# Mixture-of-experts stage of a four-layer network on one core: transposes by DMA in place of TensorE

## What is computed

```python
logits = xf @ gate_inp.T
topv, topi = jax.lax.top_k(logits, K)             # K = 4 of E = 16 experts
w = jax.nn.softmax(topv, axis=-1)
u = jnp.einsum('nc,ehc->neh', xf, W_up)           # C = 256, H = 448
g = jnp.einsum('nc,ehc->neh', xf, W_gate)
h = jax.nn.silu(g) * u
y = jnp.einsum('neh,ech,ne->nc', h, W_down, dense_w)
```

## Time and profile before

| | |
|---|---|
| median of 3 runs | 2166.65 us |
| profiled execution, own time | 2164.68 us |
| its span in the profile | 2162.4 us |
| PE busy | 1870.4 us, 86% |
| DVE busy | 1362.2 us, 63% |
| POOL busy | 825.9 us, 38% |
| ACT busy | 761.3 us, 35% |

### The profile page before, as it was taken

How to read it: one execution, slowest core, us unless ns; L and a number is a source line. 1 busy time by engine, 2 the same in 40 slices (tenths; PEclk the granted TensorE clock), 3 DMA queues, 4 the chain that set the end, 5 groups by cost and what they waited for, 6 DMA issues and landing times. The chain is left out here.

```text
span 2162.4 us, 35897 instructions
## 1 busy us (share of the span) xinstructions
PE 1870.4 (86%) x9588; PEld 1324.7 (61%) x9589; DVE 1362.2 (63%) x3020; ACT 761.3 (35%) x1527; POOL 825.9 (38%) x823
## 2 busy tenths in 40 slices
PE   3589999999999999989999988637999999999990
PEld 2367766766666756667766756525666666666660
DVE  3778887877887877878877874213444444444445
ACT  3334434434434434434434432212222222232323
POOL 2123333332242332243332230124555555555554
PEclk7799999999999999999999998869999999999995
DMA  8223123123133223133123120068333333333337
GB/s 282 61 78 105 52 86 102 53 83 102 43 94 102 58 78 102 41 94 103 50 87 102 46 78 24 15 213 254 59 58 63 59 59 59 59 59 60 59 53 238
DMA packets 155390, 187.60 MB, mean 87 GB/s; under 512 B 38672, under 2 KB 134224, under 8 KB 154960
## 3 DMA queue, kind: packets, MB, share of 16 engines
q1 hardware_dynamic: 110288, 115.44, 17.1%
q0 software_dynamic: 40704, 67.40, 15.4%
q10 hardware_dynamic: 4352, 4.20, 0.6%
HBM read 119.23 MB, written 67.73 MB: 86 GB/s over the span
## 5 line engine op out<-in xcount | busy, mean ns | idle before, releaser
L1619 PE MATMUL pu<-w_ug,xh 128*128 x1728 | 361.7, 358 | 20.6 <-issue 11.8
L1758 POOL DMA_INDIRECT sums_dram<-yo,meta_in x144 | 227.2, 1578 | 255.8 <-DVE yo L1728 245.0
L1712 DVE TENSOR_TENSOR gate_hid<-pu,gate_hid 128x448 f32<-128x448 f32 x144 | 89.9, 625 | 361.3 <-ACT gate_hid L1680 361.3
L1619 PEld LDWEIGHTS pu<-w_ug,xh 128*128 128x128 bf16 x1728 | 169.2, 99 | 169.8 <-issue 46.1
L1680 ACT ACTIVATE gate_hid<-pu 128x448 f32<-128x448 f32 x144 | 78.4, 545 | 455.8 <-PE pu L1619 437.9
L793 PE MATMUL pb<-x1T,w_sw 128*128 128x256 f32 x1024 | 231.8, 383 | 0.7 <-ACT x1T L911 0.7
L793 PEld LDWEIGHTS pb<-x1T,w_sw 128*128 128x128 f32 x1024 | 193.7, 191 | 47.3 <-issue 15.5
L1645 PE MATMUL py<-w_dn,hh 112*128 x1728 | 215.4, 275 | 1.1 <-DVE yo L1728 1.1
L1645 PEld LDWEIGHTS py<-w_dn,hh 112*128 112x128 bf16 x1728 | 168.5, 98 | 22.1 <-issue 1.8
L1748 POOL DMA_INDIRECT xin<-x_dram,meta_in x144 | 142.2, 987 | 71.5 <-issue 42.9
L609 PE MATMUL pa<-w_in,xT 128*128 128x512 f32 (+1 forms) x384 | 155.7, 551 | 14.6 <-DMA xT<-in_xT 13.9
(11 more groups left out here) (246 smaller groups left out, 3458.7 us busy)
## 6 DMA issues: line engine op xcount, KB each, us to landing
w_stage<-in_w_ug SPq DMA_DIRECT2D x64, 224.0 KB
split_ug<-w_parts SPq DMA_DIRECT2D x64, 224.0 KB
w_ug<-split_ug SPq DMA_DIRECT2D x16, 896.0 KB, 13.5
xg_dram<-xg SPq DMA_DIRECT2D x16, 512.0 KB, 3.5
rows<-sums_dram SPq DMA_DIRECT2D x32, 256.0 KB, 5.5
w_stage<-in_w_dn SPq DMA_DIRECT2D x32, 224.0 KB
split_dn<-w_parts SPq DMA_DIRECT2D x32, 224.0 KB
w_dn<-split_dn SPq DMA_DIRECT2D x16, 448.0 KB, 14.5
```

The source lines that it names most:

```text
L1619: last = mm(pu[:, 2 * b + w, 0:EH], xh[:, b, xp, c, :], w_ug[:, bass.ds(e, 1), wp, c, w * EH:(w + 1) * EH], start=n == 0, stop=n == 3 * DC ...
L1758: nc.gpsimd.indirect_dma_start(out=sums_dram[m % 2], out_offset=bass.IndirectOffsetOnAxis(ap=meta[:, m, 0:1], axis=0), in_=yo[:, m % 2, :] ...
```

## The change

The transposes of the expert stage leave TensorE. x3 is split into its bf16 halves in `layers_block` (POOL, new piece C7), and stored so (SP, new piece C9); the gather fetches 512 bf16 values a token. The product h is split from SBUF into `hs` (padded with zeros from 112 to 128 columns a part), by ACT and DVE. SP turns both with `dma_start_transpose`: `xin` 128 x 512 bf16 into `xh`, two tiles ahead, and `hs` 128 x 1024 bf16 into `hh`, in the tile's own step. `down` is three tiles behind, the scatter four, the gather four ahead, meta five ahead. Gate comes before up in `up_gate`, with an increment after each. `xin`, `xh`, `hh` and `yo` become rings of four (`xin` was one too), `hid` single, `py` double; `UN` is 16.

```diff
-UN = 8
+UN = 16
+XS = 4
+WS = 4
-    "SP": ("C7 A0 N0 A2 WL.0 WL.1 WL.2 WL.3 WL.4 WL.5"),
+    "SP": ("C7 A0 N0 A2 WL.0 WL.1 C9 WL.2 WL.3 WL.4 WL.5"),
-    "POOL": ("A6- A2 A2L AX.0 AX.1 B2 G1+ B3 D8+ A5 B6"),
+    "POOL": ("A6- A2 A2L AX.0 AX.1 C7 B2 G1+ B3 D8+ A5 B6"),
-    x3_dram = nc.dram_tensor("x3_dram", [ntok, D], F32).ap()
+    x3_dram = nc.dram_tensor("x3_dram", [ntok, 2 * D], BF16).ap()
...
+            def store_parts(s):
+                sp.wait_ge(x3_split.sem, x3_split.at(s))
+                sp.dma_start(x3_dram[bass.ds(s * T, T), :].rearrange("(t p) d -> p t d", p=P),
+                             x3_parts[:, :, :, :].rearrange("p t h d -> p t (h d)")).then_inc(x3_stored.sem, 16)
...
+            def c7(s):
+                pool.wait_ge(x3_ready.sem, x3_ready.at(s))
+                if later(s):
+                    pool.wait_ge(x3_stored.sem, x3_stored.before(s))
+                nc.gpsimd.tensor_copy(x3_parts[:, :, 0, :], x3[:, :, :]).then_inc(x3_split.sem, 1)
+                pool.wait_ge(x3_split.sem, x3_split.at(s, 1))
+                nc.gpsimd.tensor_tensor(x3_parts[:, :, 1, :], x3[:, :, :], x3_parts[:, :, 0, :], ALU.subtract
+                                        ).then_inc(x3_split.sem, 1)
...
-        xin = sb("xin", [P, XS, D])
-        xh = sb("xh", [P, 2, 2, DC, P], BF16)
+        xin = sb("xin", [P, XS, 2 * D], BF16)
+        xh = sb("xh", [P, XS, 2 * DC, P], BF16)
+        hid = sb("hid", [P, EH])
+        hs = sb("hs", [P, 2, 2, EJ, P], BF16)
+        hh = sb("hh", [P, XS, 2 * EJ, P], BF16)
+        yo = sb("yo", [P, XS, D])
...
+            def turn_x(r, m):
+                i, b = UN * r + m, m % XS
+                if later(i, XS):
+                    sp.wait_ge(ug_done.sem, ug_done.at(i - XS))
+                    carrier.take()
+                sp.wait_ge(x_in[b].sem, x_in[b].at(turn(r, m)))
+                carrier.take()
+                sp.dma_start_transpose(xh[:, b, :, :], xin[:, b, :]).then_inc(x_turned[b].sem, 16)
+
+            def turn_h(r, m):
+                i, b = UN * r + m, m % XS
+                if later(i, XS):
+                    sp.wait_ge(down_done.sem, down_done.at(i - XS))
+                    carrier.take()
+                sp.wait_ge(h_split.sem, h_split.at(i))
+                carrier.take()
+                sp.dma_start_transpose(hh[:, b, :, :], hs[:, m % 2, :, :, :].rearrange("p h j l -> p (h j l)")
+                                       ).then_inc(h_turned[b].sem, 16)
...
             def step(r, m):
-                parts(r, m, 4, run=load_meta)
+                if not isinstance(r, int) or UN * r + m + 5 >= 4:
+                    parts(r, m, 5, run=load_meta)
+                parts(r, m, 2, run=turn_x)
+                parts(r, m, 0, run=turn_h)
                 if isinstance(r, int) and 3 <= UN * r + m + 4 < NE:
                     load_weights(UN * r + m + 4)
...
-                pe.wait_ge(x_split.sem, x_split.at(i))
+                pe.wait_ge(x_turned[m % XS].sem, x_turned[m % XS].at(turn(r, m)))
...
-                for w in range(2):
+                for w in (1, 0):
...
-                pe.wait_ge(h_split.sem, h_split.at(i))
-                if later(i):
-                    pe.wait_ge(y_ready.sem, y_ready.before(i))
+                pe.wait_ge(h_turned[m % XS].sem, h_turned[m % XS].at(turn(r, m)))
+                if later(i, 2):
+                    pe.wait_ge(y_ready.sem, y_ready.at(i - 2))
...
                 parts(r, m, 0, run=up_gate)
-                parts(r, m, -1, run=transpose_h)
-                parts(r, m, 2, run=transpose_x)
-                parts(r, m, -2, run=down)
+                parts(r, m, -3, run=down)
...
                 parts(r, m, 0, run=gate_part)
-                parts(r, m, -1, run=h_part)
-                parts(r, m, 2, run=x_part)
+                parts(r, m, 0, more=h_part)
...
+                act_f(hs[:, m % 2, 0, :, 0:EC], hid[:, :].rearrange("p (j l) -> p j l", j=EJ), ACT.Copy
                       ).then_inc(h_high.sem, 1)
...
+                vec.tensor_tensor(hs[:, m % 2, 1, :, 0:EC], hid[:, :].rearrange("p (j l) -> p j l", j=EJ),
+                                  hs[:, m % 2, 0, :, 0:EC], ALU.subtract).then_inc(h_split.sem, 1)
...
                 parts(r, m, 0, run=hidden)
-                parts(r, m, -1, run=h_part)
-                parts(r, m, 2, run=x_part)
-                parts(r, m, -2, run=y_part)
+                parts(r, m, -3, run=y_part)
+                parts(r, m, 0, run=h_part)
...
+                if later(i, 2):
+                    pool.wait_ge(y_stored[m % 2].sem, y_stored[m % 2].at(pair(r, m) - 1))
+                    carrier.take()
                 pool.wait_ge(y_ready.sem, y_ready.at(i))
...
-                parts(r, m, -3, run=scatter)
-                parts(r, m, 3, run=gather)
+                parts(r, m, -4, run=scatter)
+                parts(r, m, 4, run=gather)
```

More of the change, by code:

```diff
@@ L1488, in experts_block @@
         meta = sb("meta_in", [P, UN, 4], U32)
[L1489 to L1505 removed]
+        xin = sb("xin", [P, XS, 2 * D], BF16)
+        xh = sb("xh", [P, XS, 2 * DC, P], BF16)
+        gate = sb("gate", [P, EH])
+        hid = sb("hid", [P, EH])
+        hs = sb("hs", [P, 2, 2, EJ, P], BF16)
+        hh = sb("hh", [P, XS, 2 * EJ, P], BF16)
+        yo = sb("yo", [P, XS, D])
+        pu = ctx.enter_context(nc.psum_tensor("pu", [P, 4, 512], F32))
+        py = ctx.enter_context(nc.psum_tensor("py", [P, 2, 512], F32))
+        weights_in = [sig(f"weights_in{n}", 32) for n in range(WS)]
         meta_in = [sig(f"meta_in{n}", 16) for n in range(XS)]
         x_in = [sig(f"x_in{n}", 16) for n in range(XS)]
[L1508 to L1511, removed]
+        x_turned = [sig(f"x_turned{n}", 16) for n in range(XS)]
+        ug_done = sig("ug_done", 2)
         gate_ready = sig("gate_ready", 1)
         hid_ready = sig("hid_ready", 1)
[L1514 removed]
+        rest_cleared = sig("rest_cleared", 1)
         h_high = sig("h_high", 1)
         h_split = sig("h_split", 1)
+        h_turned = [sig(f"h_turned{n}", 16) for n in range(XS)]
         down_done = sig("down_done", 1)
@@ L1519, in experts_block, with turn, pair @@
         y_stored = [sig(f"y_stored{n}", 16) for n in range(2)]
+        def turn(r, m):
+            return UN // XS * r + m // XS
+        def pair(r, m):
+            return UN // 2 * r + m // 2
         def steps(eng, run, first, last):
@@ L1622, in up_gate @@
                             n += 1
[L1623 to L1633, removed]
+                    last.then_inc(ug_done.sem, 1)
             def down(r, m):
                 i = UN * r + m
-                b = m % 2
-                e = expert_of(step_at[0], step_at[1], -2)
-                pe.wait_ge(h_split.sem, h_split.at(i))
-                if later(i):
-                    pe.wait_ge(y_ready.sem, y_ready.before(i))
+                e = expert_of(step_at[0], step_at[1], -3)
+                pe.wait_ge(h_turned[m % XS].sem, h_turned[m % XS].at(turn(r, m)))
+                if later(i, 2):
+                    pe.wait_ge(y_ready.sem, y_ready.at(i - 2))
                 n = 0
@@ L1665, in _ @@
             act_f = nc.scalar.activation
[L1667 to L1673, removed]
+            carrier = Carrier(act, waited)
             def gate_part(r, m):
                 i = UN * r + m
-                act.wait_ge(ug_done.sem, ug_done.at(i))
+                act.wait_ge(ug_done.sem, ug_done.at(i, 1))
                 if later(i):
                     act.wait_ge(hid_ready.sem, hid_ready.before(i))
-                act_f(gate, pu[:, 2 * (m % 2) + 1, 0:EH], ACT.Silu).then_inc(gate_ready.sem, 1)
+                act_f(gate[:, :], pu[:, 2 * (m % 2) + 1, 0:EH], ACT.Silu).then_inc(gate_ready.sem, 1)
             def h_part(r, m):
                 i = UN * r + m
-                act.wait_ge(h_transposed.sem, h_transposed.at(i))
+                if isinstance(i, int) and i == 0:
+                    act.wait_ge(rest_cleared.sem, rest_cleared.at(0))
                 if later(i, 2):
-                    act.wait_ge(down_done.sem, down_done.at(i - 2))
-                act_f(hh[:, m % 2, 0, :, :].rearrange("p j l -> p (j l)"), ph[0:EC, m % 2, :], ACT.Copy
+                    before = turn(r + (m - 2) // UN, (m - 2) % UN)
+                    act.wait_ge(h_turned[(m - 2) % XS].sem, h_turned[(m - 2) % XS].at(before))
+                    carrier.take()
+                act.wait_ge(hid_ready.sem, hid_ready.at(i))
+                act_f(hs[:, m % 2, 0, :, 0:EC], hid[:, :].rearrange("p (j l) -> p j l", j=EJ), ACT.Copy
                       ).then_inc(h_high.sem, 1)
@@ L1699, in _ @@
             vec = nc.vector
[L1700 to L1705, removed]
+            carrier = Carrier(dve, waited)
             def hidden(r, m):
                 i = UN * r + m
+                if later(i):
+                    dve.wait_ge(h_split.sem, h_split.before(i))
+                    carrier.take()
+                dve.wait_ge(ug_done.sem, ug_done.at(i))
```

(2 more changed lines are left out.)

79 lines of the change are left out of this document (36 added, 43 removed).

## The result

The changed kernel takes 2225.05 us (median of 4, 2220.64 to 2227.14) where the kernel before takes 2167.31 us. The ratio is 1.0281, with a 95% interval of 1.0256 to 1.0306. The forecast of 2156 us had the wrong sign; the result lies in the stated range of 2080 to 2250, between A and C. The profiled execution took 2225.38 us with a span of 2223.6, against 2164.68 and 2162.4: 61.2 us more span.

What follows compares the result with a forecast made beforehand. The PE bounds the kernel before at 4.47 us a tile; SP was to bound the changed one at 4.27. Terms -25, +12 and +2 gave -11 us, 2153.7 profiled, 2156 as median, range 2080 to 2250.

Steps and rivals of the forecast that it cites:

- A: The forecast itself: in the expert stage SP becomes the bound near 4.27 us a tile, 2156 us (2125 to 2190); chance 0.45.
- C: Expert stage: each transposing DMA holds SP 1.58 us like POOL's scatter, 5.03 us a tile, 2250 us; chance 0.30.
- What bounds the kernel, and what the PE gives up: Expert stage: the PE bounds at 4.47 us a tile; dropping six transposes takes off 0.81, leaving a floor of 3.66.
- The price of a transposing DMA on SP: Expert stage: each transposing DMA holds SP 1.2 us, taken near POOL's indirect DMAs because it cuts rows in small pieces.
- 1.47 + 0.4: SP's work per tile besides the transposing DMAs: 1.47 us for meta, 0.4 for the turns' waits and increments.
- The sign of being wrong: Forecast wrong if a transfer's hold is under 1.0 or over 1.4 us, or the last steady wait is not on a turn.
- The DMA engines: Expert stage: the turns add 1.2 to 2.4 us a tile, 2.9 to 4.1 in all, busy but under SP's 4.27.
- rival B: Expert stage: transposing DMAs hold SP like plain ones, the PE stays the bound at 3.66 to 3.95, 2082 us; chance 0.20.
- Rival D: DMA engines: 256-byte pieces cost far more than their bytes, 12.8 us a tile, 2300 us or more; chance 0.05.
- POOL's waits, ACT and DVE in the expert stage: Per tile DVE needs 1.8 us, ACT 1.1, POOL about 3.2, all hidden behind the PE's 3.66; POOL's extra wait causes no stall.
- Start of the stage: Start of the expert stage: turns share SP's queue with the weights and add 0 to 25 us, taken as +12.
- Layers: Layers block: POOL's split of x3 takes 2.3 us 16 times, hidden in POOL's idle time, so 0; uncovered 37 us.

Runs made afterwards that it cites:

- plain_row: Changed kernel with both transposing DMAs replaced by plain row copies, data left untransposed: 2073.76 us in one run, against 2156.49 for the kernel before.
- un16: Kernel before with only the expert loop lengthened from 8 to 16 tiles a round: 2133.18 us against 2149.47, ratio 0.9915.
- h_only: Changed kernel with only h turned by DMA; x transposed on the PE and the layers block as in the kernel before: 2084.01 us, ratio 0.9655 to the kernel before.
- plain_256: Changed kernel with both transposing DMAs replaced by plain copies in 256-byte pieces, data left untransposed: 2104.25 us in one run, against 2156.49 for the kernel before.
- x_pair: Changed kernel with the x of two tiles turned by one transposing DMA: 2160.83 us against 2161.49 for the kernel before, ratio 0.9989.
- meta_act: Changed kernel with the meta load issued by ACT in place of SP: 2116.29 us against 2156.49 for the kernel before, ratio 0.9811.

## Why the prediction was wrong

**What bounds the kernel, and what the PE gives up**: the bound was right, the number in part by luck. With SP out of the way (plain_row) the pace is 3.70 us, forecast 3.66. But the six transposes were priced at 0.81 us by their weight loads, and the median tile falls only from 4.24 us (before and un16) to 3.59 (plain_row), by 0.65; the four of h bring it to 3.80 (h_only), 0.44 in place of 0.53. The loop of 16, which I priced at nothing, gave 0.12 back, and the two errors nearly cancel.

**The price of a transposing DMA on SP**: right, 1.22 and 1.24 us for the 1.2 that I took between POOL's rows. But my reason, the number of pieces, was wrong: plain_256 has the pieces and holds SP 0.60 us, x_pair has twice the bytes and no longer hold. The number came from POOL's DMAs, which are another kind, so that it fits is luck.

**The step that failed** is the rest of SP's sum, "1.47 + 0.4". Measured it is 4.78 - 1.22 - 1.24 = 2.32 us, 0.45 more, and 124 x 0.45 = 56 us of the 69 between 2156 and the result. (With the means of the turns, 1.13 and 1.25 us, some being recorded late and short, the rest is 2.40.) The waits and increments of the turns take about 0.3 us and more before each in place of 0.2. The meta part is longer too: 1.2 to 1.5 us ahead of its DMA of 0.35, where 1.47 us had been for all of it. One piece of that is the register load itself, 0.27 us before and 0.37 after at the median; why it is slower is open:

```profile
L1558 SPq TENSOR_LOAD <-table x101: 262/268/283, 1600.1 to 2047.1; - x101
L1579 SPq TENSOR_LOAD <-table x94: 28/370/769, 1602.3 to 2048.1; - x94
```

So SP needs 4.78 us a tile, above the 4.47 of the kernel before, where I had 4.27 and 0.20 us of gain in hand. That is less than the uncertainty of a sum of a dozen small instructions on an engine with no slack; the sum had no bounds of its own, while the DMA's price had. The sign of being wrong that I wrote down, a hold under 1.0 or over 1.4 us, did not show either: it watched the term that came out right.

**That SP becomes the bound** (case A's mechanism): right, shown by meta_act and x_pair, which take work from SP, turn the same bytes and run at 4.0 and 4.25 us a tile. Rival C named this side for another reason, a longer hold, which did not come; its 5.03 us a tile lies 0.25 above the 4.78 that was measured, and comes near it by another term.

**The DMA engines**: I forecast 1.2 to 2.4 us a tile for the turns. In the changed kernel q1 takes 41.5% of 400 us over 84 tiles, 1.98 us, less 0.07 for meta as before: 1.9 us for 393 thousand bytes, 206 GB/s. "Busy, but not the bound" was right there, and it is probably what stops meta_act at 4.0 us: its share is 0.98. Taking the load off SP thus did not reach rival B's 3.66 to 3.95 us; the h-only form with two thirds of the bytes gets to 3.92. The page "DMA: Bandwidth & Descriptors" of the Trainium skill (Latency and other measured facts) gives 261 GB/s for a transpose with a non-contiguous middle dimension; the 206 measured here, beside the gathers and scatters, are below it.

```profile
q1 hardware_dynamic: 145427, 32.97, 41.5%
q0 software_dynamic: 16128, 22.03, 37.7%
```

**Rival D**: wrong; q1 with all its 256-byte pieces takes 1.80 us a tile in plain_256 and 1.98 in the changed kernel, not 12.8.

**POOL's waits, ACT and DVE in the expert stage**: hidden, as said. POOL waits 83.2 us for meta data in 450 us, since SP is late.

**Start of the stage**: +12 forecast, about +10 in the profiled pair (8.6 before the first up_gate and the 2.2 by which 40.2 exceeds 38). That the two are near is luck: the 8.6 us are there because the first turn of x stands behind the weights of three experts. I had named that queue and priced only the bytes.

**Layers**: 0 forecast, 5 to 7 us measured for C7 and C9 alone. The cover was real for POOL, which was idle; I looked at the engine that does the work and not at the one that shares its way to SBUF.

**UN = 16** I priced at nothing; alone it gains 16 us (2133.18 against 2149.47). That gain is in the PE's stalls, which are hidden where SP is the bound, so how much of it the changed kernel has is not known.

## What to carry over

Before work is moved to a sequencer, add up its whole step (waits, increments, register loads) and not only the new DMAs: here SP's small instructions and its meta load cost 2.32 us a tile, nearly as much as the two turns with 2.46. A transposing DMA was paid for by the DMA, so few and large ones were right here, and the part that frees most of the bound engine for least of the new one (h: four transposes for one DMA) should go first, alone. For work given to an idle POOL, look at what DVE does with two SBUF inputs at the same time. And before a body in a loop is compared with another, measure its first and last step apart from the others.

## What the runs showed of the hardware that I had not expected

A transposing DMA of 128 KB and one of 256 KB both hold SP's sequencer about 1.2 us, a plain one of the same bytes 0.47, and 0.60 in 256-byte pieces. The turns cost the DMA engines 1.9 us a tile, plain copies in 256-byte pieces 1.73 (1.80 less meta's 0.07) and in rows of 1 and 2 KB 1.13: most of what a turn costs there over a plain copy in long rows is the price of small pieces (q1 has 1731 packets a tile in the changed kernel, 1701 in plain_256). A turn of 128 KB issued behind the weights of two more experts let the PE start 8 us later than one issued ahead of them. And each turn of the expert loop cost the PE some 1.5 us at its first and last tile, so that a loop body of twice the length took 0.12 us off every tile.
